# Value products of an attention layer: V held in the array, transposed probabilities streamed, and a new order table

## The reference

```python
# layer 1, "attn": a selective state-space scan (DI=512 channels, 16 states)
dA = jnp.exp(d_t[..., None] * A)
h = dA * h + d_t[..., None] * b_t[:, None, :] * u_t[..., None]
y = jnp.einsum('bds,bs->bd', h, c_t)        # then + D*x, * silu(z), @ W_out
# layer 1, "ffn": two attentions of 8 heads x 64, light + heavy
attn = softmax(q @ k.T)                     # light: windows of 128 tokens
out = attn @ v                              # heavy: 256 routed queries, all 512 keys
out = out.reshape(b, n, 512) @ wo           # heavy rows are put back at their places
```

## Time and profile before

| | |
|---|---|
| Median of 3 runs | 2310.9 us (2303.4 to 2311.5) |
| Profiled execution, its own time | 2311.4 us |
| Profiled execution, span from first to last instruction | 2309.6 us |
| Busy share of the span: PE, PEld, DVE, ACT, POOL | 91%, 57%, 72%, 57%, 60% |
| Mean granted clock of TensorE, as a share of 2.4 GHz | 0.939 |
| Layer 1 from its first scan (964.9 us) to the end | 1344.7 us |

### The profile page before, as it was taken

The page is one execution under the profiler, slowest core; times in us unless marked ns, Lnnn a source line. Parts: engine busy times, 40 slices in busy tenths (PEclk is TensorE's granted clock), DMA queues, the critical chain, the costliest instruction groups (busy, mean ns, idle before and its releaser), DMA issues.

```text
span 2309.6 us, 43294 instructions
## 1 busy us (share of the span) xinstructions
PE 2104.1 (91%) x13987; PEld 1321.1 (57%) x13987; DVE 1656.2 (72%) x3057; ACT 1315.1 (57%) x2930; POOL 1391.6 (60%) x1053
## 2 busy tenths in 40 slices
PE   5999999999999955599999999999998999999986
PEld 3767667576666642265564565555555555645644
DVE  4676766657675632387897896896997887988865
ACT  4253543525355322467668668667668676777653
POOL 3232432424243300477887987987977977978974
PEclk9999998989999966799999999998999998999977
DMA  4001010000000031523543542533623524534320
GB/s 117 11 29 37 5 35 9 31 15 25 29 9 22 11 112 39 154 66 109 141 109 91 147 106 88 156 87 94 173 74 116 156 73 131 131 95 134 100 65 19
DMA packets 111152, 181.73 MB, mean 79 GB/s; under 512 B 25513, under 2 KB 62281, under 8 KB 110929
## 3 DMA queue, kind: packets, MB, share of 16 engines
q1 hardware_dynamic: 110928, 178.95, 27.7%
HBM read 132.17 MB, written 46.73 MB: 77 GB/s over the span
## 4 chain that ended last, share of the span: by engine, by line
PE 39%; ACT 6%; issue 6%; POOL 5%; DVE 4%; DMA 1%; SPq 0%; POOLq 0%; ACTq 0%; DVEq 0%
PE bank L1584 34%; PE bank L1672 4%; POOL HB L1532 4%; DVE bank L1957 1%; ACT bank L1815 1%; ACT PT L1762 1%; PE bank L1695 1%; POOL Sel L1550 1%; ACT SD L1798 1%; ACT SD L1786 1%; POOL HB L1538 1%; DVE HB L1957 1%; ACT PR L1853 1%; ACT SD L1894 1%; DVE Sel L1945 1%
## 5 line engine op out<-in xcount | busy, mean ns | idle before, releaser
L1532 POOL TENSOR_TENSOR HB<-DD,BC 128x512 f32<-128x512 f32 x512 | 644.4, 1288 | 139.7 <-PE bank L1584 126.5
L1815 ACT ACTIVATE bank<-DD,A 128x512 f32<-128x512 f32 x512 | 348.9, 690 | 138.0 <-DVE HB L1957 79.4
L1538 POOL TENSOR_TENSOR HB<-HB,BC 128x512 f32<-128x512 f32 x256 | 327.5, 1285 | 85.6 <-DVE HB L1957 85.4
L1957 DVE TENSOR_TENSOR_SCAN HB<-bank,HB 128x512 f32<-128x512 f32 x256 | 310.9, 1214 | 94.6 <-ACT bank L1815 55.2
L1957 DVE TENSOR_TENSOR_SCAN bank<-bank,HB 128x512 f32<-128x512 f32 x256 | 312.0, 1219 | 85.8 <-POOL HB L1532 42.8
L417 POOL TENSOR_TENSOR hr<-hs,half 128x16 f32<-128x16 f32 x32 | 94.5, 2952 | 277.6 <-DVE hs L927 277.6
L1584 PEld LDWEIGHTS bank<-Va,PT 128*128 128x128 f32 x1536 | 200.0, 204 | 68.7 <-issue 50.4
L442 PE MATMUL bank<-W,XT 128*128 128x512 f32 x512 | 231.2, 597 | 1.1 <-ACT QT L690 1.1
L1584 PE MATMUL bank<-Va,PT 128*128 128x64 f32 x1536 | 212.8, 289 | 4.7 <-ACT PT L1762 3.3
L716 ACT ACTIVATE HS<-bank,SC 128x128 f32<-128x128 f32 x256 | 73.0, 368 | 197.6 <-PE bank L442 197.6
L1962 DVE TENSOR_TENSOR HB<-bank,BC 128x512 f32<-128x512 f32 x256 | 173.9, 679 | 7.8 <-DVE bank L1957 0.5
(11 more groups left out here) (232 smaller groups left out, 4094.0 us busy)
## 6 DMA issues: line engine op xcount, KB each, us to landing
DD<-dd_scratch SPq DMA_DIRECT2D x512, 128.0 KB, 3.3
BC<-ssm_scratch SPq DMA_DIRECT2D x128, 128.0 KB, 3.2
US<-us_scratch SPq DMA_DIRECT2D x32, 512.0 KB, 3.5
us_scratch<-U SPq DMA_DIRECT2D x8, 1024.0 KB, 4.2
us_scratch<-SD SPq DMA_DIRECT2D x8, 1024.0 KB, 6.5
dd_scratch<-SD SPq DMA_DIRECT2D x8, 1024.0 KB, 4.3
dd_scratch<-U SPq DMA_DIRECT2D x8, 1024.0 KB, 6.5
XI<-in_L_attn_x SPq DMA_DIRECT2D x8, 512.0 KB, 4.0
```

Source lines behind the costliest of these rows:

```text
L1532: done(pool.tensor_tensor(HB[:, c % HR], du, bc, ALU.mult), "dbu")
L1538: done(pool.tensor_tensor(h, h, bc, ALU.mult), "cg")
L1815: done(act.activation(PD[n % 2][:], delta, ACT.Exp, scale=A[:, k:k + 1]), "dA")
L1957: done(dve.tensor_tensor_scan(h if n % 2 else dA, dA, h, 0.0, ALU.mult, ALU.add), "scan")
```

## The change

- `value` takes two items (two heads) at a time. 64 columns of V are held in the array and a block of PT, 128 columns, is streamed. The head of even parity goes to the array's columns and the bank's partitions 0 to 63, the odd one to 64 to 127. The result comes out transposed, channels on the partitions, as `widen` wants it. There are 12 `value` steps a batch, of 8 matmuls each.
- `oturn` and `oturnc` and the tile O are gone. The reciprocals have a step of their own (`rec`, DVE). `spread` (PE) multiplies each reciprocal, repeated over 64 columns, with the identity: 8 matmuls a tile, into a bank of the rotation; `spreadc` (ACT) copies the result to RS; `norm` (DVE) multiplies the bank of the values with RS into OT.
- PT has four buffers in place of two. DT becomes the same tile as SSM, and `ssmc` also waits for the readers of DT of the batch before. `zc` also waits for `ssq`.
- All of `AT` is new, and PERIOD is 170.44 in place of 170.64.

```diff
-PERIOD = 170.64
+PERIOD = 170.44
...
+def pairs_of(a):
+    return sorted({m // 2 for m in items_of(a)})
...
-        U, SD, SSM, DT = sb("U", [NB, T]), sb("SD", [NB, T]), sb("SSM", [T]), sb("DT", [T])
+        U, SD, SSM = sb("U", [NB, T]), sb("SD", [NB, T]), sb("SSM", [T])
+        DT = SSM
-        PR, PT = sb("PR", [2, T]), sb("PT", [2, T])
+        PR, PT = sb("PR", [2, T]), sb("PT", [4, T])
-        O, OT = sb("O1", [HIDA]), sb("OT1", [HIDA])
+        OT, RS = sb("OT1", [HIDA]), sb("RS", [HIDA])
...
-                def value(b, m):
+                def value(b, i):
...
                     for j in range(4):
-                        if m < 2 * NT:
-                            h = m % 2 + 2 * j
-                            q = mm(PB[6 + a % 2][:, h * DH:(h + 1) * DH], PT[:, m % 2, j * P:(j + 1) * P],
-                                   V[:, m // 2, h * DH:(h + 1) * DH])
...
+                        for par in range(2):
+                            half, pt = slice(DH * par, DH * (par + 1)), PT[:, (2 * i + par) % 4, j * P:(j + 1) * P]
+                            if i < NT:
+                                h, cols, kv = par + 2 * j, slice(j * P, (j + 1) * P), i
+                            else:
+                                pair = (i - NT) % (AH // 2)
+                                h, cols, kv = par + 2 * pair, slice(pair * P, (pair + 1) * P), j
+                            q = mm(PB[6 + a % 2][half, cols], V[:, kv, h * DH:(h + 1) * DH], pt,
+                                   i < NT or j == 0, i < NT or j == 3)
                     done(q, "value")
-                def turn_out(b, a):
+                def spread(b, a):
+
+                    after(pe, "rec", b, a)
+                    bank = claimed(pe, "spread", b, a)
+                    for j in range(NA):
+                        for par in range(2):
+                            q = mm(bank[DH * par:DH * (par + 1), j * P:(j + 1) * P],
+                                   rec[:, a, 2 * j + par:2 * j + par + 1].broadcast_to([P, DH]), ident[:])
+                    done(q, "spread")
...
                 def turned(b, m):
-                    after_item(act, "value", ITEMS * b + m - 2)
-                    copied(PT[:, m % 2], "turn", b, m, "turnc")
+                    after_values(act, ITEMS * b + m - 4)
+                    copied(PT[:, m % 4], "turn", b, m, "turnc")
...
-                def turned_out(b, a):
-                    after(act, "oturn", b, a)
+                def spread_out(b, a):
...
+                    copied(RS[:], "spread", b, a, "spreadc")
...
-                    done(dve.tensor_tensor(O[:].rearrange("p (h d) -> p h d", h=AH),
-                                           PB[6 + a % 2][:].rearrange("p (h d) -> p h d", h=AH), bc(rec[:, a], DH),
-                                           ALU.mult), "norm")
+                    done(dve.tensor_tensor(OT[:], PB[6 + a % 2][:], RS[:], ALU.mult), "norm")
```

More of the change, by code:

```diff
@@ new lines @@
+    "in": [-112.81, -107.81, -103.85, -96.74],
+    "cinit": [-111.6, -106.34, -101.8, -92.22],
+    "conv": [-111.3, -110.3, -107.47, -106.27, -103.62, -102.74, -99.38, -98.17, -92.39, -88.28, -86.48, -84.83],
+    "z": [-106.86, -100.25, -89.8, -91.44],
+    "zc": [-106.3, -94.23, -84.17, -85.87],
+    "silu": [-80.97],
+    "us_st": [-68.99],
+    "ssm": [-62.43],
+    "ssmc": [-61.67],
+    "ssm_st": [-58.17],
+    "dt_ld": [-55.48],
+    "abs": [-46.21, -53.17, -52.98, -52.16],
+    "sexp": [-38.32],
@@ new lines @@
+    "relu": [-27.91, -29.26, -45.18, -38.21],
+    "sln": [-36.93],
+    "del": [-26.14, -33.14],
+    "du": [-23.11, -23.32],
+    "dd_st": [-16.29],
+    "xrt": [-55.66, -59.42],
+    "xrtc": [-54.86, -58.48],
+    "k_ld": [-65.29],
+    "rank": [-32.6, -18.15, -17.01, -22.87],
+    "ranks": [-10.01],
+    "sel": [29.9, -7.16, 26.75, -3.43],
+    "proj": [-8.74, -12.55, -13.14, -17.02, -17.39, -10.83, -11.55, -10.8, 8.73, 7.24, 20.04, 1.73, 46.97, 52.57,
+        68.9, 76.55, 61.09, 85.73, 94.0, 104.89, 99.62, 98.34, 90.32, 94.29],
@@ L1214 @@
+    "tail": [187.64, 196.03, 196.44, 205.66],
+    "tailc": [188.21, 197.41, 200.71, 207.89],
+    "out": [202.26, 204.05, 206.02, 209.26],
+    "x_ld": [50.19],
 }
@@ L1321, in after_item, with after_values @@
                 after(eng, kind, *divmod(n, ITEMS))
+        def after_values(eng, n):
+            if n >= 0:
+                after(eng, "value", *divmod(n // 2, ITEMS // 2))
         def after_exp(eng, n):
@@ L1746, in _ @@
                         value(b, i)
-                    elif what == "oturn":
-                        turn_out(b, i)
+                    elif what == "spread":
+                        spread(b, i)
                     elif what == "widen":
@@ L1792, in ssm @@
                         act.wait_ge(over["ssm_dma"], 16 * b)
+                    after(act, "abs", b - 1, *range(NB))
+                    after(act, "relu", b - 1, *range(NB))
                     done(act.activation(SSM[0:2 * DS + 1], banks.of["ssm", b, 0][0:2 * DS + 1], ACT.Copy), "ssmc")
@@ L1820, in project @@
                     if kind and what == "v":
-                        after(act, "value", b, *range(2 * NT))
+                        after(act, "value", b, *range(NT))
                     elif kind:
@@ L1824, in project @@
                     elif what == "v":
-                        after(act, "value", b - 1, *range(2 * NT, ITEMS))
+                        after(act, "value", b - 1, *range(NT, ITEMS // 2))
                     else:
@@ L1879, in _ @@
                             act.wait_ge(over["del_dma"], 16 * b)
+                        after(act, "ssq", b, *range(NT))
                         copied(SD[:, i], "z", b, i, "zc")
@@ L1909, in _ @@
                         heavy(b, i)
-                    elif what == "oturnc":
-                        turned_out(b, i)
             @block.vector
@@ L1981, in largest, with reciprocals @@
                     done(q, "max")
+                def reciprocals(b, a):
+                    for m in items_of(a):
+                        after_exp(dve, ITEMS * b + m)
+                    after(dve, "spread", b - 1, a)
+                    done(dve.reciprocal(rec[:, a], sums[:, a]), "rec")
                 def normalise(b, a):
-                    after(dve, "value", b, *items_of(a))
+                    after(dve, "value", b, *pairs_of(a))
+                    after(dve, "spreadc", b, a)
                     if a:
-                        after(dve, "oturn", b, a - 1)
+                        after(dve, "widen", b, a - 1)
                     else:
-                        after(dve, "oturn", b - 1, TILES - 1)
-                    own.now(dve.reciprocal(rec[:, a], sums[:, a]))
-                    done(dve.tensor_tensor(O[:].rearrange("p (h d) -> p h d", h=AH),
-                                           PB[6 + a % 2][:].rearrange("p (h d) -> p h d", h=AH), bc(rec[:, a], DH),
-                                           ALU.mult), "norm")
+                        after(dve, "widen", b - 1, TILES - 1)
+                    done(dve.tensor_tensor(OT[:], PB[6 + a % 2][:], RS[:], ALU.mult), "norm")
                 def widened(b, a):
@@ L2032, in _ @@
                         largest(b, i)
+                    elif what == "rec":
+                        reciprocals(b, i)
                     elif what == "norm":
```

146 lines of the change are left out of this document (55 added, 91 removed), and 43 rows, old and new, of the table AT.

## The result

| | before | after |
|---|---|---|
| Median on the same chip | 2311.2 us (4 runs, 2303.4 to 2313.0) | 2224.5 us (4 runs: 2247.2, 2201.8, 2201.2, 2250.2) |
| Profiled execution, its own time | 2311.4 us | 2247.2 us |
| Profiled execution, span | 2309.6 us | 2245.5 us |

The change makes the kernel faster: the ratio is 0.956, 95% interval 0.950 to 0.962. The changed kernel has two levels of time, one from 2201 to about 2225 us and one from 2247 to 2256; the ratio is formed from the lower level alone (2201.8, 2201.2 and a fifth run of 2220.2 us), the median contains both (as a ratio 0.962), and the profile shows an execution of the upper one. I forecast 2262 us with a range of 2230 to 2300, so the gain was larger than the range allowed, by 5.5 us.

The account below looks back on a forecast made before the run. TensorE's queue was taken to bound the kernel. Eight batches at -4.2 us for the products, -11 for the silu wait and -4 at the start gave -49: 2311 to 2262 us, range 2230 to 2300.

Parts of the forecast that it names:

- The terms for the order: New order table: -11 us from TensorE's wait behind silu and -4 us at the start; the rest left unpriced.
- the silu wait: TensorE's 3.1 us wait before the ssm product, behind ScalarE's silu block: about half goes, -1.5 us in seven batches, -11.
- the start: Start of layer 1: BC loads moved ahead of dd_st, half the selections behind the first products; -4 us, once.
- The term for the products: TensorE's matmuls per batch: 11.2 for values, 5.6 for spreads, 2.0 for switches, less 23.0 removed; -4.2 us, eight times.
- the removed value groups: TensorE's 24 old value groups of 8 instructions a batch, priced at 0.85 us each, 20.4 us saved.
- The added groups: TensorE's 12 new value and 6 spread groups of 16 instructions a batch, 0.93 us each (0.86 to 0.99).
- Rival 3: Array halves don't run side by side at 128 columns: 1.71 us a group, 2374 us; chance 0.03.
- rivals 1 and 4: 1: another engine, GpSimdE, holds the period, 2286 us, chance 0.14; 4: new order makes TensorE wait, 2358 us, chance 0.08.
- the 20 us stretch without a fold: TensorE's longest stretch between folds, now folds 5 to 6, 20.2 us against about 17 before; could make GpSimdE wait; unpriced.
- The condition that I wrote for the prediction being wrong: TensorE's idle time in a period growing from 10 to over 17 us would show the prediction wrong.
- my third condition: Prediction wrong if longer waits lower TensorE's granted clock; periods at 0.95 cost 4.4 us more than one at 1.00.
- Rival 2: New order also removes most of TensorE's waits, 3 of 10.3 us a period; 2238 us, chance 0.08.

Follow-up runs that it names:

- e11: Kernel before, with the rank step's second VectorE instruction reading one SBUF input in place of two; 2296.9 us, ratio 0.996.
- e13: Kernel before's products in the new order table, with the rank step's second instruction on one SBUF input; 2248.1 us, ratio 0.974.
- e5: Changed kernel, with the rank step's second VectorE instruction reading one SBUF input in place of two; 2171.8 us, ratio 0.941.
- e6: Changed kernel with the value step's loops swapped, all four blocks of the even head, then the odd one's; 2213.7 us, ratio 0.962.
- e3: Kernel before with the new products, spread and copy into RS, in the old order table; 2369.5 us, ratio 1.025.
- e8: Against e3, rec and spread a little earlier, the copy into RS further behind the spread; 2337.8 us, ratio 1.014.
- e9: Against e8, every value pair moved 1.2 later in TensorE's queue, behind the next score; 2344.4 us, ratio 1.017.
- e4: Changed kernel with the keys of rank steps 0 and 3 moved later, behind GpSimdE's run of del and du; 2205.7 us, ratio 0.953.
- e12: Changed kernel with the reference's result, no two-SBUF-input VectorE rank instruction, equal keys masked within the block on GpSimdE; 2182.7 us, ratio 0.947.

## Why the prediction was right or wrong

The direction, the engine that bounds, and the mechanism (halves side by side) were right. What failed is the size of two terms of the sum, and one loss had no term at all:

- The terms for the order, -15 us (-11 for the silu wait, -4 for the start, which was right); it measured -49 (e11 to e13).
- The term for the products, 8 x -4.2 = -34 us; it measured -76 (e13 to e5). The step in it that was mis-sized is the price of the removed value groups.
- The two-input VectorE instruction, at nothing; it takes back 38 us at the lower level and more at the upper one.

One by one:

- **The added groups: right.** I forecast 0.93 us a value group (0.86 to 0.99) plus a switch of 0.10. Rows of after:

```profile
1441.00 1.09 PE L1595 MATMUL bank<-PT,Va 128*64 128x128 f32 x16
1441.93 1.04 PE L1595 MATMUL bank<-ident,rec 128*64 128x128 f32 x16
1442.80 1.04 PE L1595 MATMUL bank<-PT,Va 128*64 128x128 f32 x16
1443.77 1.16 PE L1595 MATMUL bank<-Ka,Qa 64*128 64x128 f32 x16
```

   A spread takes 0.87 when a value follows, a value 0.93 when a spread follows and 0.97 to 1.03 with a switch behind it. Rival 3 (one after the other, 1.71 us) is refuted by these rows, and e6 shows what in-turn order costs: 1.51.

- **The removed groups: the term of the sum that was mis-sized.** I priced 24 old value groups at 0.85 us, 20.4 a batch, from the row of 0.84 and a pair of 1.74. Read over a whole period (1308 to 1474 us of before), the first starts give 0.92 to 1.13 for most of them, where a group of another form or a wait follows, and two of the 24 run at the lower clock:

```profile
1435.74 1.88 PE L1584 MATMUL bank<-Va,PT 128*128 128x64 f32 x8
1437.55 2.08 PE L1584 MATMUL bank<-Ka,Qa 64*128 64x512 f32 x4
1439.56 1.97 PE L1584 MATMUL bank<-Va,PT 128*128 128x64 f32 x8
1441.45 1.08 PE L1584 MATMUL bank<-HB,fold 128*32 128x512 f32 x4
```

   All 24 together take 24.7 us, the switches at their ends included (a part of which the 2.0 us for switches counts again). With that the sum for a batch would have been 11.2 + 5.6 + 2.0 - 24.7 - 2.6 = -8.5 us, and TensorE's busy time fell by 8.3 (156.2 to 147.9). I had taken the cheapest neighbour for the groups that go, and typical ones for those that come. Of the 4.3 us that I missed, 1.6 are the lower clock, so they are no work saved: in the period from 1974 us, all of it at full clock, the 24 groups take 23.0.

- **The silu wait: right in kind, too small.** I forecast that half of the 3.1 us in front of ssm goes. In after it is there in the first batch alone; idle time before that group over the whole kernel fell from 27.9 to 5.8 us:

```profile
L1595 PE MATMUL bank<-U,Wx 128*33 128x512 f32 x64 | 31.8, 643 | 5.8 <-ACT SD L1803 5.8
```

   That is -22, where I had -11.

- **The start: right.** I forecast -4 us, and the 11.4 us by which the first scan comes earlier seem to say more. But 5.3 of them are not layer 1's. From layer 1's first table load to its first scan the traces with the old table take 75.1 to 77.5 us (before, e3, e8, e9, e11) and those with the new one 70.7 to 72.9 (after and the others): about 4 us. Most of it is where I put it, between the store that all DD loads wait for and the first scan: 15.2 to 15.5 us with the old table, 12.6 to 12.8 with the new one. SyncE in after:

```profile
940.90 0.38 SPq L1480 DMA_DIRECT2D dd_scratch<-SD  x1
947.91 9.14 SPq L1493 DMA_DIRECT2D DD<-dd_scratch  x20
957.10 3.01 SPq L1472 DMA_DIRECT2D BC<-ssm_scratch  x6
```

   No BC load stands between the DD loads any more, as four did in the earlier trace rows.

- **The order as a whole.** "What I can't price is the rest", I wrote, and the rest was larger than what I had priced: 49 us by e11 and e13, where my terms for it were 15. The first and last batch, which alone shrink by 14 and 25 us, have no term in my sum at all: I priced every batch like a middle one.

- **The wait that took the place.** My rivals 1 and 4 had GpSimdE and the 20 us stretch without a fold in view. The stretch cost nothing visible in e5 (idle 5.8 us a period). The condition that I wrote for the prediction being wrong, idle time up from 10 to over 17 us, was nearly met (16), but through the rank instruction, on which I had no sentence. The lower clock behind a longer wait, my third condition, did appear (0.50 from 1578.0 to 1588.1 us), though the mean of the period, 0.97, is no lower than before's. I also wrote that VectorE stays at 137 us; it went to 146.7, and that row alone pointed to the cause. The trace of before held the hint: one form of instruction whose single times go from 0.75 to 2.1 us.

- **The sum.** -49 us forecast; -125 (2297 to 2172) without the two-input instruction; with it -77 to -87 by the medians and -98 to -102 by the ratios of the lower level. A too small sum and an unseen loss partly cancelled, so that I missed the range by only 5.5 us: that the miss is so small is luck.

- **The chances.** Rival 2 (2238 us, 0.08), that the order takes away TensorE's waits as well, describes e5 best: idle time 10.3 to 5.8 us a period. In after itself no rival describes the period; the forecast's 158 to 163 us a period was missed on one side at 163.8 and on the other in e4 (157.1).

Three points stay open. What sets which level an execution of the changed kernel takes wasn't seen: both its profiles have the 11.57 us instruction, and that the two levels are this instruction is argued from their absence in e4, e5 and e12. What decides whether the instruction is held through a whole run of GpSimdE or served between two of its instructions isn't shown. And of the loss of the products in the old order, 27 of 56 us have no cause shown.

## What to carry to other kernels

Before pricing a new order, look in the trace of before for an instruction whose single times differ on one and the same shape, and ask what the other engines do in its long instances; a new order can move it from the mild form into the long one. Price what is removed with the same mean over a period as what is added, not with the cheapest neighbour, and give the first and the last batch of a pipeline terms of their own. When one instruction meets another engine's run, every experiment on timing can move that meeting: take the disturbance out first, in all versions, and compare then.

## What the runs showed of the hardware that was not expected

- A VectorE instruction with two SBUF inputs, 0.75 us by itself, took 11.57 us while GpSimdE worked without a gap; it ended 0.55 us after the last of seven GpSimdE instructions (1.24 to 2.35 us each) had ended, and 4.72 to 4.89 us over four of them in e4. With one input it took 737 to 745 ns in all 32 cases (e5). The Trainium skill (SBUF — State Buffer, Who interferes with whom) has the lock as held for one instruction; here the waiting engine wasn't served between two instructions of the other. Elsewhere, in before at 1120.48 us, it was, and the GpSimdE instruction behind took 1.71 us in place of 1.25.
- Within the 10.5 us wait TensorE's granted clock fell to 0.50, and it stayed there until 1588.1 us, 4.5 us after TensorE had gone on. So the wait costs the work behind it too: a group of turns 1.97 us in place of 1.03.
- Two halves of the array, 128 rows by 64 columns each, with 16 instructions of 128 columns, take 1.00 us when the heads alternate and 1.51 when they come one after the other (e6), and not the 1.71 of rival 3. Where these 0.2 us come from isn't shown.
